# A decoder layer's softmax sums taken by token quarter and spread by matmul, with a layer norm moved ahead of two copies

## The chip, the cores and the metric

One core of a Trainium2 chip runs the whole program. The metric is the time of one execution on the device in microseconds (us), the median of several runs. The engines are TensorE (PE in the profile, its weight loads PEld), VectorE (DVE), ScalarE (ACT), GpSimd (POOL) and SyncE (SP, which here only issues transfers). Each has its own instruction stream; semaphores order them against each other.

## The reference

One post-norm decoder layer on x of 16 sequences of 64 tokens, 128 wide, all in float32:

```
x = LN(x + attn(x))              # 16 heads of 8, causal
x = LN(x + xattn(x, ctx))        # window attention, 16 heads, keys and values from ctx
h = x + attention(rms(x)*w1)     # rope on x, 16 query heads, 4 key/value groups
h = h + moe(rms(h)*w2)           # 8 experts, top 2, SwiGLU, 512 hidden
x = LN(x + h)
```

Each attention is softmax(q k^T * scale + mask) v. The kernel divides after the product with v: output = (exp(scores) v) / (sum of exp(scores)), so it needs one sum per token and head, repeated over the 8 dimensions of the head.

## The kernel before

The 1024 tokens are 8 tiles of 128 (two sequences each). Three attention stages times 8 tiles make 24 steps, numbered 0 to 23; behind them come routing and the experts, which the change leaves alone. Each engine has one loop over the steps, written out by hand, and one iteration works on several steps at once:

- TensorE, iteration i: scores of step i (L542 adds the mask, L546 the products), turn of x of step i+2 (L494), turn of the probabilities of step i-1 (L494, two halves of four), projections of i+2 (L530 to L532), row sums (L572) and values (L579) of i-1, output projection of i-2 (L593 adds the residual in the first two stages, L595 is the product).
- ScalarE: copies the turned x (L759), takes the exponents of i-1 (L781, two halves) out of PSUM, copies keys (L771) and queries (L773) of i+2, applies the layer norm of i-3 (L802, only in the first two stages), copies the values of i+2 (L793). In the third stage it takes the square sum of i-3 first (L812).
- VectorE: reciprocal (L917) and product (L921) of i-2, statistics or residual of i-3 (L935, L939, L942), then for both halves of step i the maximum (L899) and its subtraction (L907), then rope of i-4 (L954) and the scaling by the RMS norm of i-3 (L961).
- GpSimd: the layer norm's scale of i-3 (L402 to L416, L422 to L424 in the third stage), key expansion of i+2 (L379), rope's sum (L434, L435).

Row sums and values share the PSUM bank `ps_o`: columns 0 to 127 the values, 128 to 255 the sums. The sums of step i are products of the exponents with `ones_d`, which writes each sum to the 8 rows of its head, so that the reciprocal works on 128x128 elements. TensorE may overwrite `ps_o` when the product L921 of the step before is done (`d_o`). The output projection waits for the layer norm of the step before it, which empties `ps_y` (`a_x`). Small products are placed in 32-column tiles of the array (128*32 in the profile's rows); a float32 product is two passes and so two records.

Of the kernel before, what the change touches and what calls it, by code (L numbers as in the profile page):

```python
# [21 lines left out]
P = 128  # L22
# [34 lines left out]
C_END = C_ORD + NE  # L57

def decoder_kernel(nc, t_in, consts, out):  # L60
    ctx = ExitStack()
    with ctx:
# [11 lines left out]
        ps_v = ps_xt[:, 2 * P:3 * P]  # L74

# [34 lines left out]
        ones_d = sb("ones_d", [P, 2, 32])  # L110
# [4 lines left out]
        rsum = sb("rsum", [P, 2, P])  # L115
# [64 lines left out]
        in_cst = sem("in_cst")  # L180
        in_x = sem("in_x")
# [24 lines left out]
        pe_o = sem("pe_o")  # L206
        pe_vb = sem("pe_vb")
# [7 lines left out]
        a_sq = sem("a_sq")  # L215
        d_mx = sem("d_mx")
# [62 lines left out]
        def _(sp):  # L279
# [34 lines left out]
            sp.wait_ge(c_zero, 9)  # L314
# [22 lines left out]
        def _(pool):  # L337
# [4 lines left out]
            pool.wait_ge(c_zero, 8)  # L342
# [147 lines left out]
        def _(pe):  # L490
# [24 lines left out]
            def project(n):  # L515

                s, i = n // NT, n % 2
                pe.wait_ge(a_xt, n + 1)
                if n >= 1:
                    pe.wait_ge(a_q, 2 * n)  # L520
                    pe.wait_ge(a_k, n)
                    pe.wait_ge(a_v, 4 * n)
                if n == 0:
                    pe.wait_ge(c_wq, 3)
                if n == NT:
                    pe.wait_ge(a_wx, 1)
                if n == 2 * NT:
                    pe.wait_ge(c_wkv, 2)
                kv = xt[:, i, 1 if s == 1 else 0, :]
                mm(ps_qkv[:, 0:P], w_q[:, s, :], xt[:, i, 0, :], start=True, stop=True)  # L530
                mm(ps_qkv[:, P:2 * P], w_k[:, s, :], kv, start=True, stop=True)
                mm(ps_v, kv, w_v[:, s, :], start=True, stop=True).then_inc(pe_qkv, 1)  # L532
# [28 lines left out]
            def values(n):  # L561

                i = n % 4
                pe.wait_ge(a_pt, 2 * n + 2)
                pe.wait_ge(a_v, 4 * (n + 1))
                if n >= 1:
                    pe.wait_ge(d_o, n)
                for a in range(2):
                    for j in range(4):
                        h, jj = j // 2, j % 2  # L570
                        p = pt_sb[:, h, :].rearrange("k (b j a q) -> k b j a q", b=2, j=2, a=2)
                        mm(ps_o[32 * j:32 * j + 32, P:2 * P], ones_d[:, a, :], p[:, :, jj, a, :],  # L572
                           start=(a == 0), stop=(a == 1))
                for b in range(2):
                    for a in range(2):
                        for j in range(4):
                            h, jj = j // 2, j % 2
                            c = (2 * b + jj) * P + a * S
                            k = mm(ps_o[32 * j:32 * j + 32, b * S:(b + 1) * S], vbd[:, i, b, j, a * 32:(a + 1) * 32],  # L579
                                   pt_sb[:, h, c:c + S], start=(a == 0), stop=(a == 1))  # L580
                k.then_inc(pe_o, 1)

# [50 lines left out]
            for it in range(STEPS + 2):  # L633
                if it < STEPS:
                    scores(it)
                if it + 2 < STEPS:
                    turn_x(it + 2)
                if 1 <= it <= STEPS:
                    turn_p(it - 1, 0)
                    turn_p(it - 1, 1)  # L640
                if it + 2 < STEPS:
                    project(it + 2)
                if 1 <= it <= STEPS:
                    values(it - 1)
                if 2 <= it:
                    out_proj(it - 2)
                if it == STEPS:
                    route_turn(0)
# [99 lines left out]
        def _(act):  # L748
            A = nc.scalar.activation
            act.dma_start(cst[:, :], consts).then_inc(in_cst, 16)  # L750
            for c, n in enumerate(("wq", "wk", "wv", "wo")):
                act.dma_start(wx_raw[:, c, :], t_in["L0_xattn_" + n]).then_inc(in_wx, 16)

# [29 lines left out]
            def copy_v(n):  # L783
# [3 lines left out]
                if n == 0:  # L787
                    act.wait_ge(c_zero, 8)
                if n >= 4:
                    act.wait_ge(pe_o, n - 3)  # L790
                for b in range(2):
                    for p2 in range(2):
# [4 lines left out]
                        k.then_inc(a_v, 1)  # L797

# [26 lines left out]
            for it in range(STEPS + 3):  # L825
                if it - 3 >= 2 * NT:
                    square(it - 3)
                if it + 2 < STEPS:
                    copy_xt(it + 2)
                if 1 <= it <= STEPS:  # L830
                    exponent(it - 1, 0)
                    exponent(it - 1, 1)
                if it + 2 < STEPS:
                    copy_qk(it + 2)
                if 3 <= it < 2 * NT + 3:
                    finish(it - 3)
                if it + 2 < STEPS:
                    copy_v(it + 2)
# [52 lines left out]
        def _(dve):  # L891
# [20 lines left out]
            def norm_o(n):  # L912
                i = n % 2
                dve.wait_ge(pe_o, n + 1)
                if n >= 2:
                    dve.wait_ge(d_o, n - 1)
                v.reciprocal(rsum[:, i, :], ps_o[:, P:2 * P]).then_inc(d_rs, 1)  # L917
                dve.wait_ge(d_rs, n + 1)
                if n >= 2:
                    dve.wait_ge(pe_y, n - 1)  # L920
                v.tensor_tensor(ot_sb[:, i, :], ps_o[:, 0:P], rsum[:, i, :], ALU.mult).then_inc(d_o, 1)  # L921
# [44 lines left out]
            v.memset(ones_d[:, :, :], 0.0).then_inc(c_zero, 1)  # L966
            dve.wait_ge(c_zero, 2)
            for p2 in range(2):
                for a in range(2):
                    c = p2 * 16 + a * HD  # L970
                    v.memset(ones_d[p2 * S:(p2 + 1) * S, a, c:c + HD], 1.0).then_inc(c_zero, 1)
# [15 lines left out]
            for it in range(STEPS + 3):  # L987
                if 2 <= it < STEPS + 2:
                    norm_o(it - 2)
                if it >= 3:  # L990
                    add_res(it - 3)
                if it < STEPS:
                    row_max(it, 0)
                    minus_max(it, 0)
                    row_max(it, 1)
# [201 lines left out]
def _consts():  # L1197
# [22 lines left out]
    c[:, C_ORD:C_ORD + NE] = NE - e  # L1220
    return c
# [18 lines left out]
```

## Time and profile before

| what | us |
|---|---|
| median of 3 runs | 274.57 (273.5 to 274.61) |
| profiled execution | 272.73 |
| its span, first to last instruction | 270.8 |
| PE, DVE, ACT, POOL busy | 195.1, 189.5, 118.3, 119.7 |
| granted clock, mean | 0.896 |

The attention stages fill the time to about 152 us, routing and experts the rest. Times of rows are counted from the first instruction. A row's busy time says how long an engine worked, not that anything waited for it; an idle time in brackets names who ended it.

### The profile page before, as it was taken

What the parts mean: (1) busy time and instruction counts of PE and PEld (TensorE: products, weight loads), DVE (VectorE), ACT (ScalarE), POOL (GpSimd) and SP (SyncE); (2) the same over time, 40 slices, a digit from 0 to 9 for tenths busy, and PEclk for the clock granted to TensorE, in tenths of its full rate; (3) what the DMA queues carried; (4) which work ended last, traced back from release to release, by engine and by line L of the source; (5) the groups of instructions that cost most, each with busy time, mean ns of one, the idle gap of its engine ahead of it and who ended that gap; (6) DMA issues with size and microseconds to landing.
All of it is one profiled execution on the core that took longest, in us unless ns stands there. A gap on an engine that the chain in (4) does not pass through costs nothing. (4 is left out here: it accounts for less than half of the span.)

```text
span 270.8 us, 7358 instructions
## 1 busy us (share of the span) xinstructions
PE 195.1 (72%) x2444; PEld 165.6 (61%) x2445; DVE 189.5 (70%) x458; ACT 118.3 (44%) x385; POOL 119.7 (44%) x220
## 2 busy tenths in 40 slices
PE   0488989998999899887975613499999999920000
PEld 0367877777787777665754503399999999910000
DVE  6218988788789999998994179267767766723534
ACT  1437676677567657655632220054444444400000
POOL 0216355546576766736221601454554341027771
PEclk9999999999999999999999555599999999985555
DMA  7899900000008000000000000102112223111212
GB/s 232 154 346 370 234 4 2 2 4 2 4 1 234 5 2 0 2 4 15 21 10 22 19 0 4 38 25 54 58 39 56 41 39 39 34 37 48 58 40 78
DMA packets 21339, 16.09 MB, mean 59 GB/s; under 512 B 3032, under 2 KB 18464, under 8 KB 21312
## 3 DMA queue, kind: packets, MB, share of 16 engines
q1 hardware_dynamic: 19248, 12.02, 15.5%
q0 software_dynamic: 1344, 2.76, 5.0%
q10 hardware_dynamic: 720, 0.95, 1.1%
q8 instruction: 17, 0.28, 0.4%
q14 instruction: 10, 0.08, 0.1%
HBM read 11.78 MB, written 3.93 MB: 58 GB/s over the span
## 5 line engine op out<-in xcount | busy, mean ns | idle before, releaser
L471 POOL DMA_INDIRECT early<-xm_scratch,tok_i x26 | 26.5, 1018 | 43.9 <-DMA early<-xm_scratch,tok_i 26.4
L899 DVE TENSOR_REDUCE smax<-bank 128x8 f32<-128x512 f32 x48 | 32.7, 682 | 16.2 <-PE bank L546 16.0
L691 PE MATMUL bank<-xgt,w_now 128*128 128x128 f32 x320 | 40.6, 282 | 0.4 <-ACT xgt L854 0.4
L691 PEld LDWEIGHTS bank<-xgt,w_now 128*128 128x128 f32 x320 | 38.8, 198 | 0.8 <-ACT xgt L854 0.8
L907 DVE TENSOR_TENSOR s_sb<-bank,smax 128x512 f32<-128x512 f32 x48 | 33.2, 691 | 3.2 <-PE bank L494 1.7
L379 POOL TENSOR_TENSOR k<-kt,cst 128x512 f32<-128x512 f32 x24 | 25.2, 1052 | 21.0 <-ACT kt L771 20.9
L858 ACT ACTIVATE s_sb<-bank,w_now 128x128 f32<-128x128 f32 x80 | 22.8, 367 | 23.8 <-PE bank L691 23.8
L1115 DVE SCALAR_TENSOR_TENSOR pt_sb<-bank,w_now,s_sb 128x128 f32<-128x128 f32 x80 | 22.5, 344 | 7.2 <-ACT s_sb L858 6.5
L781 ACT ACTIVATE pt_sb<-bank 128x512 f32<-128x512 f32 x48 | 26.0, 595 | 2.2 <-PE bank L494 1.8
L546 PE MATMUL bank<-k,q 64*128 64x256 f32 x192 | 26.2, 388 | 0.0
L917 DVE RECIPROCAL rsum<-bank 128x128 f32<-128x128 f32 x24 | 22.8, 951 | 3.2 <-PE bank L579 3.2
L494 PE MATMUL bank<-cst,s_sb 128*128 128x128 f32 x192 | 25.0, 273 | 0.0
L702 PE MATMUL bank<-w,pt_sb 128*128 x160 | 23.2, 288 | 0.0
L494 PEld LDWEIGHTS bank<-cst,s_sb 128*128 128x128 f32 x192 | 21.7, 141 | 0.7 <-issue 0.7
L793 ACT ACTIVATE vbd<-bank 64x64 f32<-64x64 f32 x96 | 20.8, 216 | 1.7
L759 ACT ACTIVATE xt<-bank 128x128 f32<-128x128 f32 (+1 forms) x24 | 7.5, 313 | 30.3 <-PE bank L494 30.2
L546 PEld LDWEIGHTS bank<-k,q 64*128 64x128 f32 x192 | 19.4, 194 | 1.7
L702 PEld LDWEIGHTS bank<-w,pt_sb 128*128 128x128 f32 x160 | 19.4, 191 | 1.5
L1106 DVE COPY w_now<-w_up 128x1032 f32 x22 | 15.7, 716 | 6.3 <-DVE pt_sb L1115 5.2
L773 ACT ACTIVATE q<-bank,bias_qa,cst 128x128 f32<-128x128 f32 x48 | 19.2, 455 | 0.0
L572 PE MATMUL bank<-pt_sb,ones_d 128*32 128x128 f32 x384 | 15.5, 279 | 4.8 <-ACT pt_sb L781 3.4
L483 POOL DMA_INDIRECT yg<-y_scratch,slot_i x16 | 15.1, 946 | 4.8 <-issue 4.6
(162 smaller groups left out, 347.2 us busy)
## 6 DMA issues: line engine op xcount, KB each, us to landing
w_up<-in_L_ffn_W SPq DMA_DIRECT2D x2, 2048.0 KB, 12.7
w<-in_L_ffn_W SPq DMA_DIRECT2D x8, 256.0 KB, 5.8
y_scratch<-eo SPq DMA_DIRECT2D x1, 1536.0 KB, 8.4
y_scratch<-eo SPq DMA_DIRECT2D x10, 128.0 KB
cst<-in_consts ACTq DMA_DIRECT2D x1, 672.5 KB, 4.1
early<-in_x SPq DMA_DIRECT2D x1, 512.0 KB, 6.0
early<-in_ctx SPq DMA_DIRECT2D x1, 512.0 KB, 4.8
xm_scratch<-xm SPq DMA_DIRECT2D x8, 64.0 KB, 1.5
```

Source lines behind the costliest of these rows:

```text
L379: g.tensor_tensor(k2[:, n % 3, :, :, :], kt[:, n % 2, :].rearrange("c (b u k) -> c b u k", b=2, u=1).to_broadcast([P, 2, NQ, S]), mask_p.r ...
L471: pool.indirect_dma_start(xg[:, j, :], None, xm_d[:, :], bass.IndirectOffsetOnAxis(ap=tok_i[:, j:j + 1], axis=0)).then_inc(g_gather, 16)
L494: return mm(o, i, idn, start=True, stop=True, is_transpose=True)
L546: k = mm(ps_score[h][:, b * 256:(b + 1) * 256], q2[c, i, b, :, :].rearrange("c a q -> c (a q)"), k2[c, i, b, :, :].rearrange("c p k -> c ( ...
L691: k = mm(dst[u][:, c * P:(c + 1) * P], w_now[:, u, o + c * P:o + (c + 1) * P], xgt[:, u, :], start=True, stop=True)
L702: k = mm(dst, ht[:, u, c * P:(c + 1) * P], w3[:, bass.ds(e, 1), c, :].rearrange("d a f -> d (a f)"), start=False, stop=(c == 3))
L781: A(pt_sb[:, b, :], ps_pt[b][:, :], ACT.Exp, scale=SCALE).then_inc(a_pt, 1)
L858: k = A(silu[:, u, c * P:(c + 1) * P], ps_h1[u][:, c * P:(c + 1) * P], ACT.Silu, bias=w_now[:, u, 2 * FF + c:2 * FF + c + 1])
L899: v.tensor_reduce(smax[:, b, :], ps_score[b][:, :].rearrange("q (p k) -> q p k", k=S), AX.X, ALU.max).then_inc(d_mx, 1)
L907: v.tensor_tensor(s_sb[:, b, :].rearrange("q (p k) -> q p k", k=S), ps_score[b][:, :].rearrange("q (p k) -> q p k", k=S), smax[:, b, :].re ...
L917: v.reciprocal(rsum[:, i, :], ps_o[:, P:2 * P]).then_inc(d_rs, 1)
L1115: v.scalar_tensor_tensor(ht[:, u, c * P:(c + 1) * P], ps_h2[u][:, c * P:(c + 1) * P], w_now[:, u, 2 * FF + 4 + c:2 * FF + 5 + c], silu[:, ...
```

## The change

Row sums. A token's sum no longer stands on the 8 rows of its head. The tokens of a sequence pair are cut into quarters of 32, and the sums of quarter c go to rows 2c and 2c+1 of each head, so that 32 columns hold all of them and the reciprocal works on 128x32. `ones_d` holds eight 32-column patterns for that. A second product (`spread`) with 0/1 matrices held in the constants copies each row of the reciprocal to the 8 rows of the head again, into the free columns of `ps_qkv`; ScalarE copies it to `rb_sb` (`copy_spread`), and VectorE multiplies by that copy. On VectorE the product moves from behind the reciprocal to behind the first subtraction. On ScalarE `finish` (the layer norm) now stands ahead of the query and key copies. The constants come in two transfers.

```diff
-        rsum = sb("rsum", [P, 2, P])
+        rsum = sb("rsum", [P, 2, 32])
+        rb_sb = sb("rb_sb", [P, 2, P])
...
@@ project
+                    if n >= 4:
+                        pe.wait_ge(a_rb, n - 3)
@@ values
                 for a in range(2):
-                    for j in range(4):
-                        h, jj = j // 2, j % 2
-                        p = pt_sb[:, h, :].rearrange("k (b j a q) -> k b j a q", b=2, j=2, a=2)
-                        mm(ps_o[32 * j:32 * j + 32, P:2 * P], ones_d[:, a, :], p[:, :, jj, a, :],
-                           start=(a == 0), stop=(a == 1))
+                    for c in range(4):
+                        w = (4 * a + c) * 32
+                        for j in range(4):
+                            h, jj = j // 2, j % 2
+                            p = (2 * (c // 2) + jj) * P + a * S + (c % 2) * 32
+                            mm(ps_o[32 * j:32 * j + 32, P:P + 32], ones_d[:, w:w + 32], pt_sb[:, h, p:p + 32],
+                               start=(a == 0 and c == 0), stop=(a == 1 and c == 3))
...
+            def spread(n):
+                if n == 0:
+                    pe.wait_ge(in_spread, 16)
+                pe.wait_ge(d_rs, n + 1)
+                pe.wait_ge(a_q, 2 * min(n + 4, STEPS))
+                pe.wait_ge(a_k, min(n + 4, STEPS))
+                if n >= 1:
+                    pe.wait_ge(a_rb, n)
+                for c in range(4):
+                    for j in range(4):
+                        q = slice(32 * j, 32 * j + 32)
+                        k = mm(ps_rb[q, 32 * c:32 * c + 32], cst[q, C_E + 32 * c:C_E + 32 * c + 32],
+                               rsum[q, n % 2, :], start=True, stop=True)
+                k.then_inc(pe_rb, 1)
@@ TensorE's loop
                     turn_x(it + 2)
+                if 2 <= it:
+                    spread(it - 2)
                 if 1 <= it <= STEPS:
                     turn_p(it - 1, 0)
@@ ScalarE
-            act.dma_start(cst[:, :], consts).then_inc(in_cst, 16)
+            act.dma_start(cst[:, 0:C_E], consts[:, 0:C_E]).then_inc(in_cst, 16)
...
+            act.dma_start(cst[:, C_E:C_END], consts[:, C_E:C_END]).then_inc(in_spread, 16)
...
+            def copy_spread(n):
+                act.wait_ge(pe_rb, n + 1)
+                if n >= 2:
+                    act.wait_ge(d_o, n - 1)
+                A(rb_sb[:, n % 2, :], ps_rb, ACT.Copy).then_inc(a_rb, 1)
...
                     copy_xt(it + 2)
+                if 2 <= it < STEPS + 2:
+                    copy_spread(it - 2)
                 if 1 <= it <= STEPS:
                     exponent(it - 1, 0)
                     exponent(it - 1, 1)
-                if it + 2 < STEPS:
-                    copy_qk(it + 2)
                 if 3 <= it < 2 * NT + 3:
                     finish(it - 3)
                 if it + 2 < STEPS:
+                    copy_qk(it + 2)
                     copy_v(it + 2)
@@ VectorE
-            def norm_o(n):
+            def recip_o(n):
                 i = n % 2
                 dve.wait_ge(pe_o, n + 1)
                 if n >= 2:
-                    dve.wait_ge(d_o, n - 1)
-                v.reciprocal(rsum[:, i, :], ps_o[:, P:2 * P]).then_inc(d_rs, 1)
-                dve.wait_ge(d_rs, n + 1)
+                    dve.wait_ge(pe_rb, n - 1)
+                v.reciprocal(rsum[:, i, :], ps_o[:, P:P + 32]).then_inc(d_rs, 1)
+
+            def norm_o(n):
+                i = n % 2
+                dve.wait_ge(a_rb, n + 1)
...
-                v.tensor_tensor(ot_sb[:, i, :], ps_o[:, 0:P], rsum[:, i, :], ALU.mult).then_inc(d_o, 1)
+                v.tensor_tensor(ot_sb[:, i, :], ps_o[:, 0:P], rb_sb[:, i, :], ALU.mult).then_inc(d_o, 1)
...
-                    norm_o(it - 2)
+                    recip_o(it - 2)
                 if it >= 3:
                     add_res(it - 3)
                 if it < STEPS:
                     row_max(it, 0)
                     minus_max(it, 0)
+                if 2 <= it < STEPS + 2:
+                    norm_o(it - 2)
+                if it < STEPS:
                     row_max(it, 1)
                     minus_max(it, 1)
```

Left out of the diff: the semaphores' declarations, the memsets that fill `ones_d`, the counts that wait for them, and the host's lines that fill the new constants.

## Rows read from the trace of the kernel before

**Rows 1.** Busy time by stretch: start:end, length, busy us of each engine (records), clock, DMA.
```profile
40.00:82.00 42.00, 38.69 (x619) 31.64 (x611) 34.05 (x65) 28.52 (x89) 24.39 (x56) 1.00 0.01 4
82.00:104.00 22.00, 20.09 (x357) 16.41 (x345) 21.35 (x40) 15.27 (x49) 15.02 (x39) 1.00 0.25 72
```

**Rows 2.** Who waited for whom from 60 to 82 us: total, times, longest.
```profile
PEld bank L593 <- ACT x L802: 2.0, 4, 0.5
```

**Rows 3.** Time line of one steady step: start, us, engine, line, operation.
```profile
78.50 0.39 PE L542 MATMUL bank<-mask_bf,same_q 64*128 64x512 bf16 x2
...
79.68 0.33 PE L494 MATMUL bank<-cst,x 128*128 128x128 f32 x1
...
79.96 1.04 PE L494 MATMUL bank<-cst,s_sb 128*128 128x128 f32 x8
...
80.35 0.26 POOL L406 TENSOR_SCALAR rstd<-mv,rstd 128x1 f32<-128x1 f32 x1
80.59 1.09 ACT L781 ACTIVATE pt_sb<-bank 128x512 f32<-128x512 f32 x2
80.67 0.69 DVE L907 TENSOR_TENSOR s_sb<-bank,smax 128x512 f32<-128x512 f32 x1 [0.18 <-PE bank L494]
...
81.73 0.64 PE L572 MATMUL bank<-pt_sb,ones_d 128*32 128x128 f32 x16
...
82.20 0.63 PE L579 MATMUL bank<-pt_sb,vbd 128*32 128x64 f32 x32
...
82.65 0.46 ACT L802 ACTIVATE x<-bank,rstd 128x128 f32<-128x128 f32 x1
...
83.17 0.49 PE L593 MATMUL bank<-early,cst 128*128 128x128 f32 x2 [0.34 <-ACT x L802]
...
83.81 0.39 PE L542 MATMUL bank<-mask_bf,same_q 64*128 64x512 bf16 x2
```

**Rows 4.** Busy time in single VectorE steps, from one reciprocal to the next.
```profile
94.84:100.45 5.61, 5.20 (x85) 4.22 (x81) 5.47 (x11) 3.52 (x11) 3.90 (x10) 1.00 0.02 3
117.30:124.00 6.70, 5.55 (x84) 4.50 (x84) 5.58 (x12) 3.47 (x12) 2.48 (x6) 1.00 0.00 1
128.79:133.59 4.80, 4.76 (x77) 3.72 (x77) 4.70 (x10) 3.48 (x13) 1.79 (x3) 1.00 0.05 14
```

**Rows 5.** The reciprocals: the page's group of L917, and the row of line L1096.
```profile
L917 DVE RECIPROCAL rsum<-bank 128x128 f32<-128x128 f32 x24 | 22.8, 951 | 3.2 <-PE bank L579 3.2
...
L1096 DVE RECIPROCAL rv<-rv x1: 204/204/204, 169.3 to 169.3; 128x8 f32<-128x8 f32 x1
```

**Rows 6.** Time line of a step of the third stage.
```profile
130.72 0.28 ACT L759 ACTIVATE xt<-bank 128x128 f32<-128x128 f32 x1
...
132.49 0.63 PE L579 MATMUL bank<-pt_sb,vbd 128*32 128x64 f32 x32
...
133.05 0.49 PE L595 MATMUL bank<-w_o,ot_sb 128*128 128x128 f32 x2
```

**Rows 7.** Records started by TensorE alone: L579, L572 (four), L667.
```profile
76.88:77.33 0.45, 0.45 (x32) 0.45 (x32) 1.00 0.00 0
...
76.41:76.45 0.04, 0.03 (x4) 0.03 (x5) 1.00 0.00 0
...
159.35:159.54 0.19, 0.19 (x8) 0.19 (x8) 0.50 0.00 0
```

**Rows 8.** Time line: scores of step 17, the long step, the last tile.
```profile
104.73 0.49 PE L542 MATMUL bank<-mask_bf,same_q 64*128 64x512 bf16 x2
...
119.40 0.69 DVE L907 TENSOR_TENSOR s_sb<-bank,smax 128x512 f32<-128x512 f32 x1
...
122.95 1.13 DVE L961 SCALAR_TENSOR_TENSOR xm<-h,rstd,w_norm 128x128 f32<-128x128 f32 x1 [1.02 <-POOL rstd L424]
124.00 0.94 DVE L917 RECIPROCAL rsum<-bank 128x128 f32<-128x128 f32 x1
...
146.38 0.96 DVE L917 RECIPROCAL rsum<-bank 128x128 f32<-128x128 f32 x1 [0.89 <-PE bank L579]
147.37 0.29 DVE L921 TENSOR_TENSOR ot_sb<-bank,rsum 128x128 f32<-128x128 f32 x1
147.58 0.28 DVE L942 TENSOR_TENSOR h<-bank,x 128x128 f32<-128x128 f32 x1
```

More of the change, by code:

```diff
@@ L56 @@
 C_ORD = C_T + 2 * NT
-C_END = C_ORD + NE
+C_E = C_ORD + NE
+C_END = C_E + 4 * 32
 def decoder_kernel(nc, t_in, consts, out):
@@ L74, in decoder_kernel @@
         ps_v = ps_xt[:, 2 * P:3 * P]
+        ps_rb = ps_qkv[:, 2 * P:3 * P]
         cst = sb("cst", [P, C_END])
@@ L109, in decoder_kernel @@
         vbd = sb("vbd", [P, 4, 2, 4, 80])
-        ones_d = sb("ones_d", [P, 2, 32])
+        ones_d = sb("ones_d", [P, 8 * 34])
         s_sb = sb("s_sb", [P, 2, 512])
@@ L180, in decoder_kernel @@
         in_cst = sem("in_cst")
+        in_spread = sem("in_spread")
         in_x = sem("in_x")
@@ L206, in decoder_kernel @@
         pe_o = sem("pe_o")
+        pe_rb = sem("pe_rb")
         pe_vb = sem("pe_vb")
@@ L215, in decoder_kernel @@
         a_sq = sem("a_sq")
+        a_rb = sem("a_rb")
         d_mx = sem("d_mx")
@@ L312, in _ @@
                 sp.dma_start(b_row[k:k + 1, :, :], part[:, :]).then_inc(in_brow, 16)
-            sp.wait_ge(c_zero, 9)
+            sp.wait_ge(c_zero, 7)
             sp.dma_start(y_d.rearrange("(a q) e -> q a e", q=P), eo[:, :, :]).then_inc(y_zero, 16)
@@ L341, in _ @@
             pool.wait_ge(in_b, 96)
-            pool.wait_ge(c_zero, 8)
+            pool.wait_ge(c_zero, 6)
             for s in range(3):
@@ L787, in copy_v @@
                 if n == 0:
-                    act.wait_ge(c_zero, 8)
+                    act.wait_ge(c_zero, 6)
                 if n >= 4:
@@ L965, in _ @@
             v.memset(vbd[:, :, :, :, :], 0.0).then_inc(c_zero, 1)
-            v.memset(ones_d[:, :, :], 0.0).then_inc(c_zero, 1)
+            v.memset(ones_d[:, :], 0.0).then_inc(c_zero, 1)
             dve.wait_ge(c_zero, 2)
             for p2 in range(2):
-                for a in range(2):
-                    c = p2 * 16 + a * HD
-                    v.memset(ones_d[p2 * S:(p2 + 1) * S, a, c:c + HD], 1.0).then_inc(c_zero, 1)
+                v.memset(ones_d[p2 * S:(p2 + 1) * S, :].rearrange("k (m c) -> k m c", c=34)
+                         [:, :, p2 * 16:p2 * 16 + 2], 1.0).then_inc(c_zero, 1)
             v.memset(ones_bf[:, :], 1.0).then_inc(c_zero, 1)
@@ L1220, in _consts @@
     c[:, C_ORD:C_ORD + NE] = NE - e
+    j = np.arange(32)
+    for chunk in range(4):
+        c[:, C_E + 32 * chunk:C_E + 32 * chunk + 32] = ((r[:, None] % 32 // HD == j[None, :] // HD)
+                                                       & (r[:, None] % HD == 2 * chunk))
     return c
```

## The prediction

> **What bounds the kernel now.** I read the busy time by stretch first, then who waits for whom, then the time line of one steady step. The three attention stages run as 24 steps of one software pipeline, and the change touches only those. From 40 to 82 us TensorE starts work almost without a gap (38.7 of 42 us) while VectorE has 8 us free; from 82 to 104 us VectorE is the full engine (21.35 of 22 us) [rows 1], and so it is in a step of the third stage (4.70 of 4.80) [rows 4]. So there are two regimes, and a saving on VectorE is worth something in the second only.
>
> The steady step [rows 3] goes, on TensorE: turning the probabilities at 79.96, then the projections, row sums at 81.73, values at 82.20, output projection at 83.17, scores at 83.81; the scores before it began at 78.50, so a step is 5.31 us. Two points in it are waits: the sums wait for ScalarE's second exponent (80.59 + 1.09 = 81.68), and the output projection waits for ScalarE's layer norm L802 (82.65 + 0.46 = 83.11). The second is the largest wait of the weight loads in that stretch, 0.5 us a step [rows 2]. L802 is late only since it stands behind the key and query copies L771 and L773, which wait for nothing TensorE needs soon. In the steps with rope VectorE needs 5.61 us a step and is busy 5.47 of them [rows 4]; TensorE runs ahead at 5.2 to 5.3 until buffers stop it. One step, 117.30 to 124.00, takes 6.70 us.
>
> **Layer norm first.** Exponents end at 81.68; L802 would run 81.70 to 82.17, before the values are done. Its scale comes from GpSimd at 80.35 + 0.26 = 80.61 [rows 3], 1.1 us earlier than it is wanted, so nothing new is late there. What ends the wait next is the tile switch behind the values. Without a wait (132.49 to 133.05) it takes 0.56 us from the values' start to the output projection [rows 6]; so that one could start at 82.20 + 0.56 = 82.76 instead of 83.17. Gain 0.41 to 0.43 a step, I take 0.42, in the 16 steps that have this layer norm. Bounds: 0.34, the idle time that TensorE's own row gives, and 0.52, if the switch is free. The copies come 0.47 us later; behind them on ScalarE is only the value copy, which ends where it did. GpSimd's key expansion also comes 0.47 us later, for scores two steps on.
>
> **Row sums.** 8 products of 128 columns (16 records of two passes) become 32 of 32 columns (64 records). The same rows of the array see 2 x 128 columns before and 8 x 32 after, so the columns streamed are equal: what counts is whether a short group keeps pace. Before, 16 records of 128 columns take 0.47 us (81.73 to 82.20 [rows 3]), a group of four every 0.11 to 0.12; 32 records of 64 columns take 0.45 us [rows 7], a group every 0.056. Halved once more, 32 columns give 0.028 to 0.029. Two other costs must fit under it: the weights of a 32-column tile, and issue. Four records of a group start within 0.03 us [rows 7], so issue can keep up, just. Eight products of 8 columns, with weights for each, start within 0.19 us at a granted clock of 0.50 (1.2 GHz), at most 27 ns apart [rows 7]. So the bounds are 0.028 (0.45 us for 16 groups, as before) and 0.056 (0.90 us, 0.43 more). I take 0.030: 0.48 us, 0.02 more.
>
> The Trainium skill (TensorEngine Tiling (Array Packing), Instruction Overhead) says that each matmul carries some 60 cycles, so that a short one lasts as long as one of about 60 columns. By that the pace would be that of the 64-column groups, and the sum of this section the 0.056 end. The 8-column products here do not agree with it, and no row shows 32-column fp32 tiles; it is priced below.
>
> **Reciprocal.** 128x128 took 951 ns and 128x8 took 204 [rows 5]: 6.2 ns per column, hence 0.354 us for 32, 0.60 less on VectorE a step. The multiply (0.29, its next instruction 0.21 behind it) moves behind the first subtraction.
>
> **Spread.** New on TensorE, between the turn of x and that of the probabilities: 16 products on the diagonal 32x32 tiles, 32 records, 8 groups of four. At 0.030 that is 0.24. It changes the tiling mode twice, from and back to 128x128. What a switch costs: from the values' start to the output projection 0.56 less 8 x 0.056 is 0.11 [rows 6]; from the output projection to the scores 0.64 (83.17 to 83.81) less four passes of 0.11 leaves 0.20 for a switch and the weights exposed ahead of the first [rows 3]. I take 0.10 twice, and 0.05 for weights exposed behind it: 0.49 us a step. Bounds: 0.24, if the switches cost nothing, and 0.80 with groups at 0.056 and switches at 0.15. Nothing hides it: the turn of the probabilities behind it starts the exponent chain (0.63 from the turn to the first exponent, both done at 1.72, sums at 1.77) and the sums.
>
> Its waits: the reciprocal starts when the values have landed, near 82.9, and is done 1.6 us before the next spread (84.9); the query and key copies, which now end about where L802 starts (82.65), end near 83.2, as early. On ScalarE copy_spread stands ahead of the exponents. A 128-column copy takes 0.28 us [rows 6]; a 64-column record lasts at most 0.63 - 7 x 0.056 = 0.24 [rows 3], so the spread lands within 0.1 to 0.15 of the start of the turn of the probabilities, and the copy ends near 0.45; the exponent begins at 0.63 anyway. Hidden, nearly 0.2 to spare; were that gone it costs 0.28 a step. The multiply must be done before the next sums (they overwrite its input): subtraction at 0.71, with 0.69 for it and 0.29 for the multiply it ends at 1.69 and lands some 0.05 later, against sums at 1.77. Hidden, with little to spare; a late subtraction goes straight to the sums.
>
> **Setup.** One more 64 KB transfer, issued by ScalarE while it waits, first needed near 30 us; the memsets change by about 0.1 us among VectorE work. Nothing.
>
> **The sum.** Step of the first regime: 5.31 - 0.42 + 0.49 + 0.02 = 5.40, 0.09 more (5.29 where only x is turned, one pass of 0.11 less). The spread starts at step 2, before the first layer norm: 0.51 more there. 14 further steps at 0.08 to 0.09: the scores of step 17, at 104.73 [rows 8], come 1.7 later, 106.4. Here VectorE no longer lags: 5.61 - 0.60 is 5.0 against 5.4. From there I walk on from one turn of the probabilities to the next. Scores 18 and 19: 5.3 + 5.1 (no residual product, 0.22 less), 116.8; the turn of step 19 comes 1.84 later (1.18 for the scores, 78.50 to 79.68, 0.17 for one turn of x, which is 79.68 to 79.96 less a pass, and 0.49), 118.6. In this step the rope of the last tile must end before GpSimd makes the first third-stage scale, for which xm waits (1.02 idle, then 1.13) [rows 8]. By the rows xm ends 4.6 us after the first subtraction starts (119.40 to 124.00); with the multiply 4.8. So the reciprocal ends at 118.6 + 0.7 + 4.8 + 0.4 = 124.5 and the turn, waiting for the spread, starts at 124.9: 6.35 after the last. Then the third-stage steps, TensorE-bound: 1.77 + 0.48 + 0.56 + 0.42 + 1.18 + 0.17 + 0.49 = 5.08, then twice 4.8 without a turn of x, 3.5 without scores, and 2.95 from the turn to the last reciprocal (1.77, 0.48, 0.45 and 0.25 for landing): 146.1, against 146.38 [rows 8]. VectorE had made such a step in 4.80 [rows 4]: what the missing lag gives, the spread takes back. Last, h of the last-but-one tile starts 1.20 behind that reciprocal's start (147.58) and comes 0.5 behind it; the chain after it (square, scale, xm, h, square, scale, xm) is as before: 0.6 earlier. In all 0.9 us less in the stages; all behind is untouched. The profiled execution took 272.73 us (span 270.8): 271.8. The median of the runs, 274.57, lies 1.84 above, so I forecast 273.7.
>
> **The rivals.**
> Near even, as above, own range 271.5 to 276.5: 0.52. A tenth of a microsecond on the switches or the wait makes 2 us over 20 steps, so this case itself falls on all three sides: 0.19 faster, 0.24 within 0.5%, 0.09 slower.
> Spread nearly hidden (no switch cost, since the turn of x has just made one): 0.25 less in 22 steps, 5.5, so 268 to 269. For it: the diagonal tiles could follow each other freely. Against: each switch in these rows costs 0.1. Chance 0.17.
> Slow pace of short groups. Place: TensorE's 16 groups of sums and 8 of spread; price: 24 x 22 = 528 groups times what exceeds 30 ns; it decides from 35 ns on, where it adds 2.6 us and the sum is slower. For it: 80 more products' records a step with as many weight loads, and four starts in 0.03 us is already the pace that is wanted. Against: the same starts kept pace at 64 columns. At 40 ns it adds 5.3: 279. Chance 0.20.
> A floor under short products: a group of 32 columns lasts as long as one of 64, 0.056; 528 x 0.026 = 13.7 more, 287. The 8-column rows speak against it: 0.08. The skill's rule named above is this case.
> A wait in ScalarE's place (copy_spread pushes the exponents by its 0.28): 22 x 0.28 less the slack, some 2 to 6, 276 to 280. Chance 0.03.
>
> **How the numbers follow.** Within 0.5% (1.4 us) a measurement of this kernel can't tell from no change. Faster 0.19 + 0.17 = 0.36; same 0.24; slower 0.09 + 0.20 + 0.08 + 0.03 = 0.40. The likeliest is 273.7. The range takes the hidden spread's upper half below and the 40 ns pace above, 269 to 281; the floor at 0.056 and the rest of the fast case stay out.
>
> **What would show it.** Reciprocal 128x32 at 0.35 us. No wait of the output projection for L802. In a steady step: sums to values 0.48; last turn of x to first of the probabilities near 0.6; step 5.40 before 82 us and also in the rope steps. One long wait of the spread at step 20. If sums to values reads over 0.6 the slow pace holds; if a step reads under 5.25 the switches were free. I am wrong if the exponents wait for copy_spread, or the sums for VectorE's multiply.

## The result, and the profile after

The changed kernel takes 291.31 us (median of 4 runs, 290.35 to 292.45) against 274.03 us for the kernel before beside it (4 runs, 272.94 to 274.61): ratio 1.064, 95% interval 1.058 to 1.070. It is slower by 17 us. The forecast was 273.7 us in a range of 269 to 281; it was wrong. The profiled execution took 290.35 us, with a span of 288.5 us against 270.8.

From the page of the profile after (span, busy time by engine, granted clock over the span, the queue that brings instructions, the group of the row sums):

```profile
span 288.5 us, 11293 instructions
PE 212.9 (74%) x4364; PEld 178.9 (62%) x4365; DVE 171.9 (60%) x456; ACT 123.4 (43%) x409; POOL 119.4 (41%) x220
PEclk9999999999999869999999985559999999995555
q8 instruction: 32, 0.52, 0.7%
L582 PE MATMUL bank<-pt_sb,ones_d 128*32 128x32 f32 x1536 | 18.8, 201 | 3.5 <-ACT pt_sb L810 2.2
```

Two lines answer to lines of the kernel before that looked harmless there:

```profile
span 270.8 us, 7358 instructions
...
q8 instruction: 17, 0.28, 0.4%
```

3935 more instructions, 3840 of them passes of TensorE's small products and their weight loads, and 15 more packets of 16 KB on the queue that brings instructions: 3935 / 15 is 262 instructions to a packet.

**A steady step is as forecast but for 0.15 us.** The time line of one step of the changed kernel, answering to [rows 3]:

```profile
84.78 0.45 PE L605 MATMUL bank<-rsum,cst 32*32 32x32 f32 x32
85.16 1.09 PE L500 MATMUL bank<-cst,s_sb 128*128 128x128 f32 x8
85.31 0.28 ACT L833 ACTIVATE rb_sb<-bank 128x128 f32<-128x128 f32 x1
85.86 1.08 ACT L810 ACTIVATE pt_sb<-bank 128x512 f32<-128x512 f32 x2 [0.27 <-PE bank L500]
85.92 0.69 DVE L944 TENSOR_TENSOR s_sb<-bank,smax 128x512 f32<-128x512 f32 x1 [0.72 <-PE bank L500]
86.53 0.28 DVE L961 TENSOR_TENSOR ot_sb<-bank,rb_sb 128x128 f32<-128x128 f32 x1
86.99 0.73 PE L582 MATMUL bank<-pt_sb,ones_d 128*32 128x32 f32 x62
87.57 0.63 PE L589 MATMUL bank<-pt_sb,vbd 128*32 128x64 f32 x30
88.14 0.49 PE L619 MATMUL bank<-early,cst 128*128 128x128 f32 x2
88.25 0.36 DVE L954 RECIPROCAL rsum<-bank 128x32 f32<-128x32 f32 x1
88.78 0.39 PE L550 MATMUL bank<-mask_bf,same_q 64*128 64x512 bf16 x2
```

No wait for the layer norm is left ahead of the output projection (L619). The reciprocal takes 0.36 us. The copy of the spread values (L833) ends at 85.59, ahead of the exponent at 85.86. The sums start 1.83 after the turn of the probabilities (forecast 1.77), and from their start to the output projection it is 1.15 us, where the forecast had 0.48 + 0.56 = 1.04. The usual step takes 5.55 us (5.45 without residual), where the forecast had 5.40 and 5.29.

**The rest is stalls without a releaser.** TensorE in three places, and the busy time of a step with such a stall beside the step ahead of it, answering to [rows 4]:

```profile
80.18 0.38 PE L619 MATMUL bank<-early,cst 128*128 128x128 f32 x1
82.69 0.38 PE L619 MATMUL bank<-early,cst 128*128 128x128 f32 x1 [2.14 <-issue]
```

```profile
28.50 1.09 PE L500 MATMUL bank<-cst,s_sb 128*128 128x128 f32 x8
31.78 0.49 PE L538 MATMUL bank<-xt,w_q 128*128 128x128 f32 x2 [2.18 <-issue]
...
96.28 0.88 PE L500 MATMUL bank<-cst,s_sb 128*128 128x128 f32 x6
99.57 0.58 PE L500 MATMUL bank<-cst,s_sb 128*128 128x128 f32 x2 [2.42 <-issue]
...
101.36 1.08 PE L582 MATMUL bank<-pt_sb,ones_d 128*32 128x32 f32 x64
```

```profile
88.78:94.34 5.56, 5.49 (x160) 4.47 (x160) 4.00 (x9) 3.79 (x13) 3.81 (x10) 1.00 0.32 91
94.34:104.38 10.04, 7.62 (x159) 6.23 (x158) 4.65 (x13) 4.27 (x14) 4.54 (x12) 0.72 0.40 111
```

The first of them falls between the two passes of one product, where the program has no wait. The last falls inside a turn that had already run six of its eight passes. Behind it the granted clock is 0.50 (1.2 GHz) until 105.6 us, and the 64 sum records take 1.08 us instead of 0.73; so a step of 5.55 becomes 10.04, some 2.6 of it stall and the rest slow clock:

```profile
100.00:104.00 4.00, 4.00 (x106) 3.60 (x106) 1.57 (x4) 2.76 (x9) 1.66 (x3) 0.50 0.02 4
```

What moves while TensorE stands still at 80 us? From 78 to 82.7 us the view of DMAs has one packet in all, an instruction packet, in the slice at 79.9 us, just ahead of the stall:

```profile
GB/s 0 0 0 0 0 0 0 0 0 0 0 0 0 0 0 0 139 0 0 0 0 0 0 0 0 0 0 0 0 0 0 0 0 0 0 0 0 0 0 0
...
q8 instruction: 1, 0.02, 1.8%
```

At the stall of 96.9 us it is otherwise. All 16 DMA engines are full from 93 to 98 us, with a transfer of 1536 KB that SyncE issues (`y_scratch<-eo`, it writes zeros to the experts' output and stands in every kernel here), and the instruction packet begins at 97.13, as that ends:

```profile
93.00:97.00 4.00, 4.00 (x119) 3.17 (x109) 2.93 (x7) 2.23 (x10) 2.95 (x7) 1.00 1.03 290
...
y_scratch<-eo SPq DMA_DIRECT2D x1, 1536.0 KB, 8.3
```

### The profile page after: what moved, and what is told of

The parts are those of the page before. It is cut to its first block, busy times and chain, and to the rows that moved or that the text cites. A ratio compares the mean times of both kernels' runs of the same rounds, so it can differ in the third digit from the quotient of the medians.

```text
span 288.5 us, 11293 instructions
## 1 busy us (share of the span) xinstructions
PE 212.9 (74%) x4364; PEld 178.9 (62%) x4365; DVE 171.9 (60%) x456; ACT 123.4 (43%) x409; POOL 119.4 (41%) x220
## 4 chain that ended last, share of the span: by engine, by line
PE 61%; issue 11%; POOL 7%; DVE 7%; ACT 6%; DMA 5%; SPq 2%; POOLq 0%; ACTq 0%; DVEq 0%
PE bank L719 12%; PE bank L500 9%; PE bank L554 8%; PE bank L730 8%; PE bank L582 6%; ACT pt_sb L810 4%; POOL yg L489 4%; PE bank L589 4%; PE bank L605 3%; PE bank L550 3%; PE bank L619 3%; PE bank L621 2%; DMA early<-xm_scratch,tok_i 2%; DMA bias_col<-in_L_xattn_bv 2%; PE bank L726 1%
## 5 line engine op out<-in xcount | busy, mean ns | idle before, releaser
L500 PE MATMUL bank<-cst,s_sb 128*128 128x128 f32 x192 | 26.5, 280 | 2.4 <-issue 2.4
L554 PE MATMUL bank<-k,q 64*128 64x256 f32 x192 | 26.9, 392 | 0.6 <-issue 0.6
L500 PEld LDWEIGHTS bank<-cst,s_sb 128*128 128x128 f32 x192 | 20.7, 141 | 3.5 <-issue 2.5
L582 PE MATMUL bank<-pt_sb,ones_d 128*32 128x32 f32 x1536 | 18.8, 201 | 3.5 <-ACT pt_sb L810 2.2
L582 PEld LDWEIGHTS bank<-pt_sb,ones_d 128*32 128x32 f32 x1536 | 16.1, 112 | 8.2 <-ACT pt_sb L810 7.8
L589 PE MATMUL bank<-pt_sb,vbd 128*32 128x64 f32 x768 | 17.4, 224 | 1.0 <-issue 0.9
```

Source lines behind the costliest of these rows:

```text
L500: return mm(o, i, idn, start=True, stop=True, is_transpose=True)
L554: k = mm(ps_score[h][:, b * 256:(b + 1) * 256], q2[c, i, b, :, :].rearrange("c a q -> c (a q)"), k2[c, i, b, :, :].rearrange("c p k -> c ( ...
L582: mm(ps_o[32 * j:32 * j + 32, P:P + 32], ones_d[:, w:w + 32], pt_sb[:, h, p:p + 32], start=(a == 0 and c == 0), stop=(a == 1 and c == 3))
```

## The experiments

The first theory after the result: TensorE's instruction stream is refilled in packets of 16 KB, and the change nearly doubles what it eats: 327 TensorE instructions a step against 165 before (316 and 156 of them passes and weight loads, the rest waits and register work). At a boundary between packets the refill now comes late. Its rivals: the wait for the spread and its copies; the tile switches; the slow pace of short groups.

**Layer norm first, alone** (on the kernel before):

```diff
+                if 3 <= it < 2 * NT + 3:
+                    finish(it - 3)
                 if it + 2 < STEPS:
                     copy_qk(it + 2)
-                if 3 <= it < 2 * NT + 3:
-                    finish(it - 3)
-                if it + 2 < STEPS:
                     copy_v(it + 2)
```

> The kernel before with one edit: ScalarE's layer norm stands ahead of its query and key copies. My theory (the move is worth the wait that it ends, and the loss of the change comes from what was added to TensorE's instruction stream): the output projection no longer waits for L802, a step of the first regime falls from 5.31 to about 4.9 us, until VectorE is full (4.4 us of work without rope, 5.6 with it); only the 8 to 9 steps before the rope gain, 0.42 each, 3 to 4 us in all: ratio 0.987, about 270.5. Rival (the new order is what hurts, since keys, queries and GpSimd's expansion come later and TensorE waits for them instead): not faster than before, 274 or more. No stall of TensorE over 1.5 us before 110 us by my theory.

Measured: 270.88 us against 273.66, ratio 0.989 [0.986, 0.993], span 267.4. Its steps are 4.90 (4.79 without residual) up to step 13, 0.41 less than before: the forecast's 0.42. From there VectorE is full and the steps are 5.6 and longer. In columns as [rows 1]:

```profile
40.00:82.00 42.00, 41.45 (x657) 34.38 (x647) 37.31 (x71) 29.55 (x95) 26.17 (x59) 1.00 0.08 23
82.00:104.00 22.00, 19.95 (x314) 16.50 (x313) 21.48 (x39) 14.46 (x45) 15.67 (x40) 1.00 0.12 34
```

So this part is a gain of 2.8 us by itself, and the loss lies wholly in the other part.

**The changed kernel with the old order on ScalarE** (`copy_qk` ahead of `finish` again):

> The changed kernel with ScalarE's layer norm put back behind the query and key copies. My theory: the order is not what costs; TensorE's three stalls of 2.5 us that nobody released stay, and the wait of the output projection for the layer norm comes back in the steps that have none: 2 to 6 us slower than the changed kernel, 293 to 297. Rival (the new order costs): faster than the changed kernel, under 289.

Measured: 290.49 us, ratio 1.061 [1.053, 1.070], no slower than the changed kernel. The expectation missed. The wait is back (15 times, 3.5 us) and the steps are 5.74 and 5.85, 0.3 longer, but the three long stalls take 6.4 us for 7.7 in return, and no clock falls behind the last of them:

```profile
PE bank L619 <- ACT x L838: 3.5, 15, 0.4
...
PE bank L619 <- issue: 1.6, 1, 1.6
```

In the changed kernel, then, the layer norm's 0.4 a step buys nothing. A kernel limited by its own waits would have lost 0.3 in each of 16 steps, 4.8 us.

**Without the spread.** On the changed kernel; the multiply reads the 32 sums of a row four times over. It leaves out filling the rows of a head, so the quarters are divided by sums that are not theirs.

```diff
-                if 2 <= it:
-                    spread(it - 2)
-                if 2 <= it < STEPS + 2:
-                    copy_spread(it - 2)
...
-                v.tensor_tensor(ot_sb[:, i, :], ps_o[:, 0:P], rb_sb[:, i, :], ALU.mult)
+                v.tensor_tensor(..., rsum[:, i, :].rearrange("q (u t) -> q u t", u=1)
+                                .to_broadcast([P, 4, 32]), ALU.mult)
```

> The changed kernel without the spread on TensorE and its copy on ScalarE; VectorE multiplies by the 128x32 reciprocals themselves, repeated four times along the columns, so the rows of a head are not filled as the reference wants. 64 of the about 310 TensorE instructions of a step are gone. Theory (TensorE's stalls are refills of its instruction stream, in pieces of 16 KB): besides the 22 x 0.49 = 11 us of the spread's own time some of the stalls go, 272 to 278. Rival (only the array work counts, the stalls are something else and stay): 280 to 281.

Measured: 269.78 us, ratio 0.986 [0.976, 0.996]. Steps of 4.91 to 5.2 us with 261 TensorE instructions; 26 instruction packets. It is below both expectations. Two unreleased stalls remain, with 1.78 and 1.82 us between the starts around them:

```profile
PE bank L580 <- issue: 3.2, 2, 1.6
```

The spread has only 64 of the added records and 0.47 us of time a step. 22 x 0.47 is 10.3 us; the time fell by 21.5.

**Wide sums, with the spread.** On the changed kernel; the sums are again 8 products of 128 columns, 16 passes instead of 64. The reciprocal and the spread go on as in the change, on the first quarter's sums alone, so it leaves out the sums of the other quarters.

```diff
-                    for c in range(4):
-                        w = (4 * a + c) * 32
-                        for j in range(4):
-                            ...
-                            mm(ps_o[32 * j:32 * j + 32, P:P + 32], ones_d[:, w:w + 32], pt_sb[:, h, p:p + 32], ...)
+                    for j in range(4):
+                        ...
+                        mm(ps_o[32 * j:32 * j + 32, P:2 * P], ones_d[:, 32 * a:32 * a + 32], p[:, :, jj, a, :], ...)
```

> The changed kernel with the 8 row-sum products of 128 columns of the kernel before in place of the 32 of 32 columns; the reciprocal still takes only 32 columns and the spread stays, so the sums of the other token quarters are not used. 96 of the about 310 TensorE instructions of a step are gone, the columns streamed are the same. Theory (instruction refill and feed): sums cost 0.46 instead of 0.56 us a step (2.4 us in all) and most of the unreleased stalls of 2.5 us and the fall of the clock behind them go, 276 to 281. Rival (array work alone): 291.3 - 2.4, about 289.

Measured: 273.74 us, ratio 1.002 [0.997, 1.007], span 271.2: under its expectation, and the forecast's 273.7 for the change itself. Every wait, copy, switch and dependency of the change is in it; 96 TensorE instructions a step fewer are all that is missing (about 232 are left, 23 packets). In a step with this kernel's spread (L603), sums (L580) and values (L587) nothing differs but the last tenth:

```profile
77.08 0.45 PE L603 MATMUL bank<-rsum,cst 32*32 32x32 f32 x32
77.47 1.09 PE L500 MATMUL bank<-cst,s_sb 128*128 128x128 f32 x8
...
79.30 0.65 PE L580 MATMUL bank<-pt_sb,ones_d 128*32 128x128 f32 x16
79.76 0.63 PE L587 MATMUL bank<-pt_sb,vbd 128*32 128x64 f32 x32
80.32 0.49 PE L617 MATMUL bank<-early,cst 128*128 128x128 f32 x2
...
80.96 0.39 PE L550 MATMUL bank<-mask_bf,same_q 64*128 64x512 bf16 x2
```

One unreleased stall above a microsecond is left between 24 and 150 us, the longest it has on any line there:

```profile
PE bank L587 <- issue: 1.3, 1, 1.3
```

Set against this kernel the loss can be divided. Scores of the last step start at 156.52 us in the changed kernel and at 139.60 here, 16.9 apart. 23 steps at 0.12 for the slower sums are 2.8. The two steps with the long stalls at 80 and 97 us are 3.1 and 4.6 longer, 7.5 without their 0.12s. The remaining 6.6 lie in ten steps that are 0.2 to 1.3 us longer than here. The first of the ten, 0.9 us in the first step, is no part of the change: the kernel before has that step as long (3.96 us). In the larger of the others TensorE passes a packet boundary 0.4 to 0.8 us late, goes on at the slow clock, or, at the first boundary (29 us), stalls 1.0 us longer than here.

**Cut sums on the kernel before.** Instructions without anything else of the change: each row-sum product cut into 4 of 32 columns, same weights, same sums (261 TensorE instructions a step).

```diff
+                for c in range(4):
+                    for a in range(2):
+                        for j in range(4):
+                            p = (2 * (c // 2) + jj) * P + a * S + (c % 2) * 32
+                            mm(ps_o[32 * j:32 * j + 32, P + 32 * c:P + 32 * c + 32], ones_d[:, a, :],
+                               pt_sb[:, h, p:p + 32], start=(a == 0), stop=(a == 1))
```

> The kernel before with one edit: each of the 8 row-sum products of 128 columns is cut into four of 32 columns. Same weights, same columns, same result, same reciprocal of 128x128, no spread; only TensorE's instructions rise, by 96 a step. 
Measured: 275.67 us, ratio 1.006 [1.0025, 1.010]: between the two expectations. 26 packets, steps 5.21 and 5.32 as before, and one stall of 1.90 us that the kernel before does not have, inside the sums:

```profile
29.48 0.44 PE L573 MATMUL bank<-pt_sb,ones_d 128*32 128x32 f32 x26
31.62 0.50 PE L573 MATMUL bank<-pt_sb,ones_d 128*32 128x32 f32 x36 [1.71 <-issue]
```

96 instructions more a step are borne here, nearly. What they cost is not a price per instruction: from 165 to 261 costs 2.3 us, from 232 to 327 costs 17.6.

**Shifted boundaries.** On the changed kernel, waits that are long satisfied are put ahead of TensorE's first work, 64 in one kernel and 128 in the other. If a stall belongs to a boundary of the instruction stream, it moves to earlier records by as many instructions; if it belongs to what the program does there, it stays.

```diff
+            for _ in range(64):
+                pe.wait_ge(c_half, 1)
             pe.wait_ge(in_cst, 16)
```

> The changed kernel with 64 waits, satisfied from 1 us on, ahead of TensorE's first work, while it idles for its first input (until 7 us). They move every later instruction 64 places down the stream. Changed kernel and the one with copies first have their long stalls at the same places of the stream: behind TensorE records 211, 1575, 1944 and 3001 of products. Theory (a stall is a refill at a boundary of the stream): the stalls come 32 records of products earlier, or, if the boundary falls where TensorE has work queued, shrink; the time may move by some us either way, 284 to 296. Rival (a stall belongs to a place of the program, a wait or a transfer there): same records, same time within 1 us.

> As with 64 waits, but 128 of them. Theory: the stalls come 64 records of products earlier than in the changed kernel or shrink; 284 to 297, with up to 1 us for the longer start. Rival: same records as in the changed kernel.

Two waits become one instruction (the page counts 11325 and 11357 instructions, 32 and 64 more than 11293), so the shift is half of what the expectations had. Counted in TensorE's matmul records, which are about half of its instructions, the long stalls moved so (start to start around each):

```
            changed kernel      64 waits            128 waits
1st         211  (2.46 us)      197  (2.88 us)      181  (1.93 us)
            956  (0.80)         941  (2.26)         925  (1.72 us)
            1575 (2.52)         1559 (1.45)
            1944 (2.69)         1929 (3.12)         1913 (3.26)
            3309 (0.79)         3294 (2.28)
```

14 to 16 records for 32 instructions, 30 and 31 for 64. Both shifted kernels also have stalls over a microsecond at places where the changed kernel has none, such as record 2674 with 64 waits (2.83 us) and 306 with 128 (2.15 us), and with 128 waits the stall near 1575 is gone. The stalls now fall inside the spread and inside the values, as here with 64 waits:

```profile
96.19 0.38 PE L605 MATMUL bank<-rsum,cst 32*32 32x32 f32 x23
99.51 0.33 PE L605 MATMUL bank<-rsum,cst 32*32 32x32 f32 x9 [2.93 <-issue]
...
126.81 0.62 PE L589 MATMUL bank<-pt_sb,vbd 128*32 128x64 f32 x28
130.03 0.37 PE L589 MATMUL bank<-pt_sb,vbd 128*32 128x64 f32 x2 [2.61 <-issue]
```

The place belongs to the instruction stream: shown. The traces say it more sharply still. Number TensorE's instructions from the first, waits and register work included. In all twelve traces there are 93 gaps over 0.6 us between two of them from 24 to 150 us. For 58 the trace names another engine that ended them. The other 35 all lie behind an instruction number 193 + a multiple of 256: 449, 1985, 3265, 4033 and so on, the same numbers in every kernel, also where the product that stands there is another. That is a boundary of the 16 KB packets.

Taking the packets in order, one to a boundary, which fits through the attention stages, gives for the changed kernel (us; the last two are boundaries without a stall):

```
boundary   TensorE reaches it   packet from, to   TensorE goes on
449        29.32                29.23, 30.41      31.78
3265       80.18                79.99, 81.32      82.69
4033       96.88                97.13, 98.07      99.57
2753       72.82                68.42, 69.59      72.96
3777       92.76                88.54, 89.57      92.76
```

In all 39 such stalls from 20 to 160 us TensorE goes on 1.2 to 1.6 us behind the packet's end, and in no trace does it pass a boundary less than 2.2 us behind the packet's start. In the kernel before every packet of these stages starts 3.7 us or more before TensorE reaches its boundary. So a stall is a packet that starts too near its boundary; the packet itself is no slower there (0.9 to 1.6 us).

The times are 298.25 us (ratio 1.090 [1.081, 1.098]) and 296.29 us (1.082 [1.075, 1.090]): 32 and 64 instructions that do nothing cost 7 and 5 us, only by where the boundaries fall. The first is over its expectation, the second within it.

**Spread as four whole-array products** (4 of 128x128 weights instead of 16 on the diagonal tiles; no tile switch, 48 TensorE instructions a step fewer, 279):

```diff
                 for c in range(4):
-                    for j in range(4):
-                        ...
+                    k = mm(ps_rb[:, 32 * c:32 * c + 32], cst[:, C_E + P * c:C_E + P * c + P],
+                           rsum[:, n % 2, :], start=True, stop=True)
```

> The changed kernel with the spread as 4 products over the whole array (a 128x128 0/1 matrix each) instead of 16 on 32x32 tiles: 16 instead of 64 TensorE instructions a step and no change of the tiling mode, but eight weight loads of 128 columns, 0.11 each, about 0.87 us instead of 0.47. Theory (instruction stream counts): 0.4 x 22 = 9 us more of array time, less some 5 to 9 us of stalls, so 289 to 295 in spite of it, with fewer unreleased stalls. Rival (array time alone): 300.

Measured: 294.01 us, ratio 1.074 [1.066, 1.082]. The spread takes 0.81 us from its start to the turn behind it instead of 0.38, so the step is 5.76 to 5.87:

```profile
67.66 0.98 PE L603 MATMUL bank<-rsum,cst 128*128 128x32 f32 x8
68.47 1.07 PE L500 MATMUL bank<-cst,s_sb 128*128 128x128 f32 x8
```

That is 22 x 0.32 = 7 us of time spent to save instructions, and stalls stay: 2.53 us at 62.8 and five more of 1.0 to 1.9. The time is within its expectation, the fewer stalls that it counted on did not come, though 279 instructions in 5.87 us is a slower average than the 261 in 4.9 to 5.2 us of the kernel without spread. Average rate alone does not say where a refill comes late.

**Token halves instead of quarters.** The change with row sums by half: 16 products of 64 columns, reciprocal 128x64, spread of 8 products of 64 columns (about 231 TensorE instructions a step).

```diff
-                    for c in range(4):
-                        w = (4 * a + c) * 32
+                        for c in range(2):
+                            w = (2 * a + c) * 32
...
-                            mm(ps_o[32 * j:32 * j + 32, P:P + 32], ones_d[:, w:w + 32], pt_sb[:, h, p:p + 32], ...)
+                                mm(ps_o[32 * j:32 * j + 32, P:P + 64], ones_n[:, w:w + 32], pt_sb[:, h, p:p + 64], ...)
```

> The change made with token halves instead of quarters: 16 row-sum products of 64 columns, a reciprocal of 128x64 (about 0.55 us), a spread of 8 products of 64 columns. Same columns on TensorE as in the changed kernel, same waits, same order of ScalarE and VectorE, but about 214 TensorE instructions a step instead of 310. Theory (the instruction stream is what the change ran into; its array work and waits are as forecast): steps of 5.3 and 5.45 us and at most one or two unreleased stalls, 273 to 276, a ratio of 0.995 to 1.01. Rival (short products as such, or the spread's waits, cost the 17 us): 283 or more.

Measured: 274.65 us, ratio 1.005 [1.003, 1.007]; 23 packets, steps 5.31 and 5.41, one stall above a microsecond in the stages. Time and stalls are as expected. This is the idea of the change without its instruction count, correct and complete, and it is nearly even (0.5% slower), as the forecast was (0.3% faster): the 0.42 gained by the layer norm goes into the spread.

**Halves only where VectorE is full.** Layer norm first in all steps; halves and spread in steps 10 to 17 alone, wide sums without spread elsewhere (the kernel of halves with `N0, N1 = 10, 18` for `0, STEPS`).

> The layer norm first in all steps; row sums by token halves and the spread only in the attention of steps 10 to 17, where VectorE is the full engine, and full row sums with a 128x128 reciprocal in the other steps. Theory: steps of 4.8 to 4.9 us up to the rope as in the kernel with the layer norm first alone, 5.45 instead of 5.62 through the rope steps, and the third stage as there: 1.5 to 2.5 us better than that kernel, 268 to 269.5, ratio 0.98 to 0.985. Rival (what VectorE saves TensorE's spread and refills take back): no better than the layer norm first alone, 270.5 to 272, ratio 0.989 to 0.995.

Measured: 268.38 us against 273.01, ratio 0.984 [0.981, 0.988], span 264.8: the fastest of all, within its expectation. Columns as [rows 1]:

```profile
40.00:82.00 42.00, 41.46 (x704) 33.92 (x704) 35.38 (x70) 29.33 (x95) 26.42 (x61) 1.00 0.09 26
82.00:104.00 22.00, 20.90 (x431) 16.79 (x432) 18.29 (x41) 14.54 (x49) 15.42 (x40) 1.00 0.11 30
```

Up to 82 us it runs as the kernel with the layer norm alone; behind, VectorE is busy 18.29 of 22 us instead of 21.48, and the steps with rope take 5.31 instead of 5.62. Against the layer norm alone the gain is 2.5 us by the medians, but those runs stand beside other runs of the kernel before; by the ratios it is 1.4 us, and the intervals just overlap. The two traces agree with the smaller figure: the scores of the last step start at 133.54 for 134.84 us.

## Why the prediction was wrong

**The step that failed** is that of the row sums, in the sentence "Four records of a group start within 0.03 us [rows 7], so issue can keep up, just", and the same silence in the spread. The prediction asked whether TensorE can start instructions at that pace for a few tens of them. It never asked whether the instructions arrive. 160 more of them a step were priced by pace alone, and nothing was put down for fetching them. The row that should have raised it was on the page: 17 packets of instructions for 7358 of them. The kernel with wide sums shows it: everything else of the change costs near what the forecast said, a step 5.43 for 5.40, and the missing 17.6 us come with 96 instructions a step. That its 273.74 us meets the forecast's 273.7 to the tenth is in part luck: it has one stall of 1.5 us that nobody forecast, and the 273.7 hold 1.84 us between a profiled execution and the median, which is 0.74 here. The shifted kernels and the count of instructions show that the stalls are tied to the instruction stream and not to a wait of the program.

The Trainium skill (Runtime: NRT & Kernel Launch, Instruction fetch mechanics) says that each engine's instructions are streamed in blocks of 16 KiB, 256 instructions, and that crossing a boundary is "mostly hidden". The stalls of this trace lie whole multiples of 256 instructions apart, which agrees exactly. The hiding holds for the kernel before and fails here, at 0.7 to 2.7 us for a late one and up to 3.3 in the shifted kernels.

**Layer norm first**: right, 0.41 a step for 0.42, and no wait for it is left in the changed kernel. In the changed kernel it is worth nothing, as the order put back there shows.

**Row sums, the size**: 0.030 a group was a little low. Groups start 31.6 ns apart over the first 32 records and 33.4 ns in the rest, with longer intervals (0.04 to 0.05 us) at the start and between the halves, 34 ns in the mean; sums to values is 0.55 to 0.58 us, for 0.48. First half of one set of sums, TensorE alone with its weight loads:

```profile
86.98:87.24 0.26, 0.25 (x30) 0.25 (x33) 1.00 0.00 0
```

With the values (0.60 for 0.56) this is 0.12 a step, 2.8 us in all. That is the rival "slow pace of short groups" at about its deciding point of 35 ns; it would by itself have given 276 to 277.

**A floor under short products** (0.056 a group): ruled out, although its 287 us came nearest to the result. A time can be near for the wrong reason; the group pace tells them apart.

**Spread**: 0.38 us from its start to the turn, 0.47 from the end of the turn of x, for 0.49. Right, tile switches included, and the rival that these were free is out. The whole-array form would have been dearer.

**Reciprocal** (0.36 for 0.354), **multiply ahead of the sums** (ends at 86.81, sums at 86.99), **exponents not pushed by the copy**: right. **The long step**: 6.35 forecast, 6.35 in the changed kernel and in that with wide sums; the third-stage step 5.08 forecast, 5.10 in that with wide sums (5.64 in the changed kernel, with a boundary passed late). The walk from turn to turn was sound.

**The chances**: 0.40 was given to slower, but none of it to this mechanism, and the range ended at 281.

**Why a packet starts late** is known in part. Counted from when TensorE passes the boundary before, the next packet starts within 1.5 us in most cases, and ahead of every stall over 2 us (but those at the first boundary) 2.9 to 5.3 us later. One reason is the transfer of 1536 KB: in eleven of the twelve kernels, the one before included, an instruction packet falls due under it, and in ten of them it starts 3.8 to 5.7 us behind the last boundary. The kernel before and the one with wide sums have time to spare there and do not stall; the changed kernel stalls 2.69 us and then runs at the slow clock, together the 4.6 us that its longest step has over the one with wide sums. No run moved that transfer. The other late packets of the changed kernel come while the DMA engines are idle, at 56.24, 79.99, 125.98 and 149.86 us, 2.8 to 3.0 us behind the last boundary, and each 0.92 to 0.97 us behind the start of a step's row sums, which had waited for ScalarE's exponents.

**Still open** is what holds those back. None of the numbers tried, instructions per step, their average rate, or the burst of short products, orders all kernels: 279 instructions in 5.87 us stall, 261 in 5.0 hardly. No two instruction packets lie closer than 3.3 us in any of these traces (4.8 before, 3.7 in the changed kernel).

## What to carry to other kernels

Count the instructions of a step, not only their pace: cutting each product into four column blocks makes four of each pass and weight load. With 279 to 327 TensorE instructions in a step of 5.5 to 5.9 us several packet boundaries cost 1 to 3 us each here, in places that move with every edit; with 231 to 261 one or two did. When an idle time has no releaser and stands inside a product or a run of like products, look at the instruction queue, count the instructions between the stalls, and test it by shifting the stream. Look also for a large transfer that fills the DMA engines just then: the instructions travel on them too. Make the finer split only where the engine it relieves is the bound: halves in 8 of 24 steps won 1.4 to 2.5 us beyond the layer norm's order, quarters in all lost 17.

## What was not expected of the hardware

- A late refill can cost twice. Within the stall of 2.69 us at 96.9 us the granted clock fell to 0.50 (1.2 GHz), up to 105.6 us, which made that step 1.9 us longer still; behind the stall of 2.52 us at 80.2 us it stayed at 1.00.
- TensorE went on 1.2 to 1.6 us behind the end of the packet that it waited for, in all 39 stalls counted above.
- Matmul records on different column tiles start 6.7 ns apart at a clock of 1.00, and groups of four 32-column fp32 passes keep 31.6 to 33.4 ns, well under the 56 ns of 64 columns: no floor under short tiled products shows here.
- Two satisfied waits in a row became one instruction of the program, not two.
- A reciprocal of 128x64 took 0.54 to 0.56 us, of 128x32 0.36, against 0.95 for 128x128.
